# A transformer layer on one core: VectorE's batch work moved ahead of the low halves, seven batches of inverse roots moved to Pool, and ScalarE's copy of the value product moved behind the exponentials

## The chip, the cores and the metric

The kernel runs on one core of a Trainium2 chip. The metric is the device time of one execution in microseconds, a median over several executions. The engines are PE (matrix products), ACT (ScalarE), DVE (VectorE), POOL (GpSimd) and SP (SyncE, which here only issues transfers); each works through its own list in order, and semaphores tie the lists together.

## What is computed

A layer of attention and a mixture of experts over x of shape 8 x 512 x 128, 16 heads, a causal mask. Cut to what matters:

```
x = x + attention(layernorm(x))          # y = einsum(x, Wkqv) + bkqv; softmax(q k / sqrt(128), causal) v, then Wp, bp
x = x + experts(layernorm(x))            # a shared expert, and the top 2 of 8 by a sigmoid router
def layernorm(x, eps=1e-5): return (x - mean(x)) / sqrt(var(x) + eps)
```

## The kernel before, in words

`prepare` makes a folded 128 x 128 matrix per head and normalises the input. `body` runs one loop of slots t on every engine. A unit is one head of one batch: 8 batches x 16 heads are 128 units. Every engine's list is written slot by slot, and a table of numbers (`STEPS`, `PART_STEPS`) says in which slot each piece of rarer work stands.

In slot t of the attention part:

- PE projects unit t (`project`, L982 to L984, into bank 0), then does rare work (`after_attention`: the output product `proj` at L1074, the router's `logits` at L1096 and on, `count`, `rank`), then in every fourth slot the value product of four units (`weigh_values`, L1056), then scores of unit t - 10 (`score`, L1040 to L1042) in three pieces alternating with three pieces of the coarse scores of unit t - 1 (`score_for_max`, L1019). The coarse scores share two banks, so the third piece of a slot needs DVE to have finished with the first piece of the same slot.
- ACT copies the projection as `qh` (L1264), in slots of the value product copies that product out as `oT` (L1289), takes three exponentials of unit t - 10 (L1299), issues the store of `oT` (L1303), and has rare work: `rows<-hn` (L1252, the high half of the normalised rows), halves of expert weights (L1317), an exponential of the router's numbers.
- DVE makes the low half `ql` (L1399: the projection minus qh; it waits for qh, and PE's next projection waits for it), then `take_products` (which adds the output product to x, and makes the low half of hn at L1391), then three reductions of the coarse scores (L1427, `reduce_maxima`), then the rare work: `scale_weights` (L1476: low halves of expert weights), `after_attention` (statistics L1495, L1499, an inverse root by seed and Newton steps in 13 small instructions at L108 to L119 and L1506, the reciprocal `rinv` L1486) and `send_rows` (the router's sorting and ranking). In slots of the value product the rare work stands ahead of the reductions instead.
- POOL masks the exponentials of unit t - 10 (L914, L916), and then does rare work of the slot: `onT` (L937, the product of attention outputs and inverse sums, which `proj` needs) and `hn` (L944, four instructions, which ACT's `rows<-hn` needs), later indirect transfers.
- SP issues loads and stores in its own order. Every fourth slot it stores 16 rows `lowT` and loads them back into qh; once a batch it gathers attention outputs (L807, L808), stores and spreads the inverses (L812, L817), stores the rows (L821) and loads them transposed (L832), from which PE takes the logits.

I call a slot a value slot if t = 15 + 4g (`PV_AT`), a low slot if t = 6 + 4g (`LOW_AT`; PE turns the 16 rows there, L1215), and a plain slot otherwise. The numbers of `STEPS` count from slot 29 + 16 b of batch b, so steps 2, 6, 10 and 14 are value slots, 1, 5, 9 and 13 low slots, and the rest plain. The units end with slot 127, the scores with slot 137, and the experts' units start in slot 138.

Of the kernel before, what the change touches and what calls it, by code (L numbers as in the profile page):

```python
# [5 lines left out]
F32 = mybir.dt.float32  # L6
# [4 lines left out]
ALU = mybir.AluOpType  # L11
# [435 lines left out]
PV_AT = GROUP - 1 + LAG + 2  # L447
FFN_AT = UNITS + LAG
# [3 lines left out]
STEPS = {"rinv": 0, "mult": 2, "proj": 4, "stats": 6, "aggr": 6, "newton0": 6, "newton1": 7, "newton2": 7, "norm": 8, "split": 10, "logits": 14}  # L452
# [3 lines left out]
PART_STEPS = {"sort": 18, "weigh": 22, "count": 23, "rank": 26, "place": 26, "expert": 30, "send": 27}  # L456
LAST_PART_STEPS = {"sort": 9, "weigh": 10, "count": 11, "rank": 12, "place": 12, "expert": 13, "send": 13}
SORT_LATE = ((0, 0, 0, 1, 2, 3, 4), (0, 0, 0, 0, 1, 1, 1))


def step_at(name, b):

    if (name, b) == ("logits", B - 2):
        return step_at("rinv", b) - STEPS["rinv"] + LATE_LOGITS
    return PV_AT + H - GROUP + 2 + H * b + (STEPS if b < B - 1 else LAST_STEPS)[name]


def part_step_at(name, g):

    b = SPLITS[g][1] // TB - 1  # L470
    return step_at("rinv", b) - (STEPS if b < B - 1 else LAST_STEPS)["rinv"] + (PART_STEPS if b < B - 1 else LAST_PART_STEPS)[name]

# [31 lines left out]

W_MAX_AT, W_MAX_EVERY = 11, GROUP
# [3 lines left out]
W_SPLIT_AT, W_SPLITS = W_SHARED_AT + KINDS + 2, 2  # L509
# [7 lines left out]
def w_low_at(i):  # L517

    return W_SPLIT_AT + GROUP * (i // W_SPLITS) + W_SPLITS
# [167 lines left out]
def body(nc, m, ctx):  # L687
# [37 lines left out]
    var = sb("var2", [P, TB], F32)  # L725
    tmp = sb("tmp2", [P, TB], F32)
# [27 lines left out]
    def yg(t):  # L754
# [10 lines left out]
             "xn_ready", "xn_last_ready", "x_T", "ah_ready", "al_ready", "late_xh_ready", "late_sums_placed", "late_o_placed", "late_r_ready", "same_head_made", "v_done", "v_ready", "mh_ready", "ml_ready", "scale_chain")  # L765
# [7 lines left out]
     xn_ready, xn_last_ready, x_T, ah_ready, al_ready, late_xh_ready, late_sums_placed, late_o_placed, late_r_ready, same_head_made, v_done, v_ready, mh_ready, ml_ready, scale_chain) = (sem(n) for n in names)  # L773
# [15 lines left out]
    with nc.Block() as block:  # L789

        @block.sync
        def _(sp):
# [41 lines left out]
            for g in range(GROUPS):  # L834
# [841 lines left out]
```

## Time and profile before

| | us |
|---|---|
| median of 3 runs (731.1 to 735.19) | 731.4 |
| span of the profiled execution | 730.7 |
| attention, first unit to last (qh of slot 0 to qh of slot 127) | 29.2 to 502.3 |
| scores and value products left over | 502 to 540 |
| experts, last sums and stores | 532 to 730.7 |

The profile shows one execution. A row of the timeline gives the start, the duration, the engine, the source line, what is written and read, and in brackets how long the engine sat idle before and what ended it. PEclk is the clock that PE was granted as a share of 2.4 GHz, so 0.50 is 1.2 GHz.

### The profile page before, as it was taken

Reading aid. Unit: us, or ns where it says so; the run is one execution under the profiler, and the core shown is the slowest. Engines: PE = TensorE matmul, PEld = TensorE weight load, DVE = VectorE, ACT = ScalarE, POOL = GpSimd, SP = SyncE. Lnnn points to the kernel's source line nnn. Section 1 sums busy time; section 2 is a strip of 40 time slices with the busy share of each in tenths; the row PEclk is TensorE's granted clock in tenths of the full one; section 3 lists DMA queues with packets and bytes.
Section 4 is the critical chain, followed back from the end, with each engine's and each line's share of the span. In section 5 each row is a group of like instructions: output and inputs, shape, how many; then the busy total and the mean of one; then the engine's idle time right before and its main releaser. Section 6 shows DMA issues by size and latency. Waiting matters only on the chain.

```text
span 730.7 us, 16418 instructions
## 1 busy us (share of the span) xinstructions
PE 654.0 (90%) x5432; PEld 398.4 (55%) x5432; DVE 541.8 (74%) x1903; ACT 456.8 (63%) x816; POOL 310.2 (42%) x512
## 2 busy tenths in 40 slices
PE   7488999999999999998899999999986779899992
PEld 6264455545554554554445455455565568777652
DVE  6699877787788778788877877868546655567796
ACT  3376676767667776765676776666762545565651
POOL 4493531314123223221477522313465356565773
PEclk9699999999999999999999999999998889999997
DMA  9100443621122101221132111021444257695424
GB/s 255 53 2 20 133 128 105 175 77 45 49 74 44 32 32 42 77 70 37 49 93 85 45 51 42 17 44 64 102 107 107 73 117 145 126 164 120 110 60 126
DMA packets 102768, 60.24 MB, mean 82 GB/s; under 512 B 44568, under 2 KB 94640, under 8 KB 102688
## 3 DMA queue, kind: packets, MB, share of 16 engines
q1 hardware_dynamic: 66144, 28.22, 16.2%
q10 hardware_dynamic: 32336, 22.29, 10.4%
q0 software_dynamic: 4208, 8.69, 4.6%
q8 instruction: 47, 0.77, 0.4%
q14 instruction: 33, 0.27, 0.1%
HBM read 19.62 MB, written 30.77 MB: 69 GB/s over the span
## 4 chain that ended last, share of the span: by engine, by line
PE 63%; DVE 17%; ACT 6%; issue 6%; another core or an unknown queue 2%; POOL 1%; ACTq 0%; DVEq 0%; POOLq 0%
PE bank L1019 8%; PE bank L1040 7%; PE bank L1056 7%; PE bank L1042 6%; PE bank L1041 6%; DVE junk L1427 5%; PE bank L1136 4%; PE bank L1138 4%; PE bank L1137 4%; PE bank L982 3%; PE bank L984 3%; PE bank L983 3%; DVE ql L1399 3%; ACT p_sb L1299 2%
## 5 line engine op out<-in xcount | busy, mean ns | idle before, releaser
L1299 ACT ACTIVATE p_sb<-bank,inv_scale 128x512 f32<-128x512 f32 (+1 forms) x384 | 222.0, 614 | 40.6 <-PE bank L1042 33.3
L1427 DVE CUSTOM_DVE_ANT_0 junk<-bank,causal 128x512 bf16<-128x512 f32 (+3 forms) x512 | 221.8, 483 | 31.4 <-PE bank L1019 29.0
L914 POOL TENSOR_SCALAR_AFFINE_SELECT p_sb<-p_sb 128x384 f32<-128x384 f32 x128 | 67.0, 524 | 306.5 <-ACT p_sb L1299 305.9
L1041 PE MATMUL bank<-ql,ah 128*128 128x512 f16 (+3 forms) x512 | 153.4, 300 | 0.0
L1042 PE MATMUL bank<-qh,al 128*128 128x512 f16 (+3 forms) x512 | 153.0, 300 | 0.0
L1019 PE MATMUL bank<-ah,qh 128*128 128x512 f16 (+3 forms) x512 | 132.5, 303 | 21.8 <-DVE low L1427 20.3
L1040 PE MATMUL bank<-qh,ah 128*128 128x512 f16 (+3 forms) x512 | 147.2, 300 | 0.8 <-ACT p_sb L1299 0.8
L1399 DVE TENSOR_TENSOR ql<-bank,qh 128x512 f16<-128x512 f32 x128 | 88.5, 691 | 64.7 <-ACT qh L1264 61.3
L1264 ACT ACTIVATE qh<-bank 128x512 f16<-128x512 f32 x128 | 76.5, 597 | 62.4 <-PE bank L984 60.3
L1611 DVE SCALAR_TENSOR_TENSOR al<-bank,gu_scale,ah 128x512 f32<-128x512 f32 x69 | 51.6, 748 | 61.3 <-ACT ah L1330 41.9
L1019 PEld LDWEIGHTS bank<-ah,qh 128*128 128x128 f16 x512 | 50.1, 98 | 79.7 <-DVE low L1427 47.6
L1330 ACT ACTIVATE ah<-bank,inv_gate 128x512 f32<-128x512 f32 x69 | 47.4, 686 | 68.9 <-PE bank L1138 40.9
L962 POOL DMA_INDIRECT p_sb<-ys_dram,place x64 | 69.9, 1092 | 37.2 <-PE bank L1138 14.2
L953 POOL DMA_INDIRECT xs_dram<-rows,place x64 | 65.6, 1025 | 42.4 <-issue 14.4
L1056 PE MATMUL bank<-p_sb,v_sb 128*9 128x512 f32 (+3 forms) x1024 | 74.9, 433 | 0.3 <-POOL p_sb L916 0.3
L1040 PEld LDWEIGHTS bank<-qh,ah 128*128 128x128 f16 x512 | 50.2, 98 | 40.8 <-issue 8.3
L1042 PEld LDWEIGHTS bank<-qh,al 128*128 128x128 f16 x512 | 50.1, 98 | 25.0 <-issue 0.3
L1136 PE MATMUL bank<-mh,wh 128*128 128x256 f16 x212 | 60.3, 284 | 3.3 <-issue 1.6
L1138 PE MATMUL bank<-mh,wl 128*128 128x256 f16 x212 | 60.2, 284 | 2.1 <-issue 2.0
L1041 PEld LDWEIGHTS bank<-ql,ah 128*128 128x128 f16 x512 | 50.2, 98 | 21.7 <-issue 0.3
L1137 PE MATMUL bank<-ml,wh 128*128 128x256 f16 x212 | 60.0, 283 | 1.7 <-issue 1.7
L1174 PE MATMUL bank<-wh,qh 128*128 (+1 forms) x276 | 53.6, 227 | 6.3 <-ACT ql L1325 2.7
(247 smaller groups left out, 1130.2 us busy)
## 6 DMA issues: line engine op xcount, KB each, us to landing
o_dram<-oT ACTq DMA_DIRECT2D x32, 256.0 KB, 2.3
ys_dram<-ql ACTq DMA_DIRECT2D x25, 256.0 KB
xs_dram<-causal ACTq DMA_DIRECT2D x6, 832.0 KB, 4.8
wst<-in_Wkqv SPq DMA_DIRECT2D x8, 264.0 KB, 5.0
x_sb<-in_x SPq DMA_DIRECT2D x8, 256.0 KB, 5.8
out<-x_sb SPq DMA_DIRECT2D x8, 256.0 KB
o_all<-o_dram SPq DMA_DIRECT2D x7, 256.0 KB
r_all<-r_dram SPq DMA_DIRECT2D x7, 256.0 KB
```

The lines of the kernel that those rows point to most:

```text
L1019: last = nc.tensor.matmul(m.psum[M_BANK[n % 2]][:, at:at + w], qh[:, u % RING, i * P:(i + 1) * P], m.ah[:, seg(b, N, w)], start=True, stop ...
L1040: nc.tensor.matmul(bank, m.ah[:, keys], qh[:, s, c * P:N], start=True, stop=False)
L1041: nc.tensor.matmul(bank, m.ah[:, keys], ql[:, s, c * P:N], start=False, stop=False)
L1042: last = nc.tensor.matmul(bank, m.al[:, keys], qh[:, s, c * P:N], start=False, stop=True)
L1056: last = nc.tensor.matmul(m.psum[O_BANK][32 * j:32 * j + V1, c * P:N], m.v_sb[:, v // H * TB + c, v % H, :], p_sb[v % P_RING][:, P_AT[c]:P ...
L1136: nc.tensor.matmul(out, hi, x_h, start=True, stop=False)
L1137: nc.tensor.matmul(out, hi, x_l, start=False, stop=False)
L1138: return nc.tensor.matmul(out, lo, x_h, start=False, stop=True)
L1264: nc.scalar.activation(qh[:, t % RING, :], m.psum[Q_BANK][:, :], ACT.Copy).then_inc(qh_ready, 1)
L1299: nc.scalar.activation(p_sb[v % P_RING][:, S_AT[k]:S_AT[k] + S_WIDTH[k]], m.psum[S_BANK[k]][:, 0:S_WIDTH[k]], ACT.Exp, scale=m.inv_scale[: ...
L1399: nc.vector.tensor_tensor(ql[:, t % RING, :], m.psum[Q_BANK][:, :], qh[:, t % RING, :], ALU.subtract).then_inc(ql_ready, 1)
L1427: last = nc.vector.tensor_tensor_reduce(out=junk[:, (3 * u + k) % 2, at:at + w], in0=m.psum[M_BANK[(3 * u + k) % 2]][:, at:at + w], in1=m. ...
```

## The change

Six edits, all in the attention part:

1. DVE's rare work (`scale_weights`, `after_attention`, `send_rows`, the new `place_rows`) stands ahead of `ql` in every slot, where it stood behind the reductions (or, in value slots, between `ql` and the reductions).
2. The table puts a batch's pieces into other slots: rinv 0 to 3, mult (POOL's onT) 2 to 5, proj 4 to 6, stats 6 to 7, aggr 6 to 8, norm (POOL's hn) 8 to 9; split stays at 10, logits at 14. The router's pieces are dealt over more slots.
3. For batches 0 to 6 the 13 small DVE instructions of the inverse root give way to two on POOL, an addition and a power, ahead of hn.
4. ACT copies oT behind the three exponentials of a value slot, and issues its store right behind that.
5. ACT's halves of expert weights (24 in all, two to a group of four slots) move from a plain and a low slot to a low and a value slot; DVE's low halves of them move from a value slot (two at once) to the two plain slots behind it.
6. SP gathers the attention outputs behind the store of lowT instead of ahead of it, and spreads the inverses behind the load.

The value product is cut by a table of pieces that has one piece, so it stays whole and in its slot. The diff, cut:

```diff
+PV_PIECES = ((0, 1, 2, 3),)
+PV_LAST = len(PV_PIECES) - 1
...
 PLACE_LATE = -(-(PV_AT - LOW_AT) // GROUP)
-STEPS = {"rinv": 0, "mult": 2, "proj": 4, "stats": 6, "aggr": 6, "newton0": 6, "newton1": 7, "newton2": 7, "norm": 8, "split": 10, "logits": 14}
+STEPS = {"rinv": 3, "mult": 5, "proj": 6, "stats": 7, "aggr": 8, "newton0": 8, "newton1": 9, "newton2": 9, "norm": 9, "split": 10, "logits": 14}
...
-PART_STEPS = {"sort": 18, "weigh": 22, "count": 23, "rank": 26, "place": 26, "expert": 30, "send": 27}
-LAST_PART_STEPS = {"sort": 9, "weigh": 10, "count": 11, "rank": 12, "place": 12, "expert": 13, "send": 13}
-SORT_LATE = ((0, 0, 0, 1, 2, 3, 4), (0, 0, 0, 0, 1, 1, 1))
+PART_STEPS = {"sort": 15, "weigh": 24, "count": 23, "rank": 26, "slots": 27, "place": 28, "expert": 30, "send": 28}
+LAST_PART_STEPS = {"sort": 9, "weigh": 10, "count": 11, "rank": 12, "slots": 12, "place": 12, "expert": 13, "send": 13}
+SORT_LATE = ((0, 1, 3, 4, 5, 5, 7), (0, 0, 0, 0, 1, 1, 1))
...
-W_SPLIT_AT, W_SPLITS = W_SHARED_AT + KINDS + 2, 2
+W_SPLIT_AT, W_SPLITS = W_SHARED_AT + KINDS + 3, 2
...
-    return W_SPLIT_AT + GROUP * (i // W_SPLITS) + W_SPLITS
+    return W_SPLIT_AT + GROUP * (i // W_SPLITS) + W_SPLITS + i % W_SPLITS
...
-                if g >= PLACE_LATE and (g - PLACE_LATE) % PER_BATCH == PER_BATCH - 1:
-                    gather_products((g - PLACE_LATE) // PER_BATCH)
-                    spread_inverses((g - PLACE_LATE) // PER_BATCH)
                 sp.wait_ge(t_taken, T_TURN["low", g] + 1)
                 sp.dma_start(m.c_dram[g * GROUP * TB:(g + 1) * GROUP * TB, :], lowT[g % 2][:, :]).then_inc(low_stored, 16)
+                gathered = (g - PLACE_LATE) // PER_BATCH if g >= PLACE_LATE and (g - PLACE_LATE) % PER_BATCH == PER_BATCH - 1 else None
+                if gathered is not None:
+                    gather_products(gathered)
...
+                if gathered is not None:
+                    spread_inverses(gathered)
...
+                    pool.wait_ge(spread_known, b + 1)
+                    nc.gpsimd.tensor_scalar(pool_var[:, :], m.stats[:, seg(b, TB), 1], EPS, None, ALU.add).then_inc(var_raised, 1)
+                    pool.wait_ge(var_raised, b + 1)
+                    nc.gpsimd.tensor_tensor(m.rstd[:, seg(b, TB)], pool_var[:, :], minus_half[:, :], ALU.pow).then_inc(rstd_ready, 1)
...
-                if (g := group_at(t, PV_AT)) is not None:
-                    weigh_values(g)
+                if pieces_at(t):
+                    weigh_values(*pieces_at(t))
...
-                if (g := group_at(t, PV_AT)) is not None:
-                    act.wait_ge(pv_done, g + 1)
-
-                    if g >= 2:
-                        act.wait_ge(o_stored[g % 2], 16 * (g // 2))
-                    nc.scalar.activation(oT[g % 2][:, :], m.psum[O_BANK][:, :], ACT.Copy).then_inc(oT_ready, 1)
...
-                if (g := group_at(t, PV_AT)) is not None:
+                if (g := weighed_at(t)) is not None:
+                    act.wait_ge(pv_done, g + 1)
+                    if g >= 2:
+                        act.wait_ge(o_stored[g % 2], 16 * (g // 2))
+                    nc.scalar.activation(oT[g % 2][:, :], m.psum[O_BANK][:, :], ACT.Copy).then_inc(oT_ready, 1)
                     act.wait_ge(oT_ready, g + 1)
                     act.dma_start(m.o_dram[g * P:(g + 1) * P, :], oT[g % 2][:, :]).then_inc(o_stored[g % 2], 16)
...
+                    if b < B - 1:
+                        last.then_inc(spread_known, 1)
+                    else:
+                        post.link(last)
+                        rsqrt_seed(nc, post.link, m.stats[:, seg(b, TB), 1], var[:, :], m.rstd[:, seg(b, TB)], tmp[:, :])
...
-                    if (b := batch_at(f"newton{step}", t)) is not None:
+                    if (b := batch_at(f"newton{step}", t)) == B - 1:
...
-                if (g := part_at("rank", t)) is not None:
+                if (g := part_at("slots", t)) is not None:
...
+
+            def place_rows(t):
+                c = sort
                 if (g := part_at("place", t)) is not None:
...
-                attend(t)
-                if group_at(t, PV_AT) is None:
+                if t < FFN_AT:
+                    scale_weights(t)
+                    after_attention(t)
+                    send_rows(t)
+                    place_rows(t)
+                    attend(t)
                     reduce_maxima(t)
-                scale_weights(t)
-                feed_forward(t - FFN_AT)
-                if t >= FFN_AT:
+                else:
+                    feed_forward(t - FFN_AT)
                     take_products(t)
-                after_attention(t)
-                send_rows(t)
-                if group_at(t, PV_AT) is not None:
-                    reduce_maxima(t)
+                    after_attention(t)
+                    send_rows(t)
+                    place_rows(t)
```

Three places of the order. First ACT at the value slot 35 (batch 0, step 6), from the copy qh of that slot to the copy qh of the next; before:

```order
L1264 ACTIVATE qh<-bank 128x512
L1289 ACTIVATE oT<-bank 128x512
L1299 ACTIVATE p_sb<-bank,inv_scale 128x512 x2
L1299 ACTIVATE p_sb<-bank,inv_scale 128x256
L1303 DMA o_dram<-oT 128x512
L1264 ACTIVATE qh<-bank 128x512
```

and now:

```order
L1295 ACTIVATE qh<-bank 128x512
L1324 ACTIVATE p_sb<-bank,inv_scale 128x512 x2
L1324 ACTIVATE p_sb<-bank,inv_scale 128x256
L1330 ACTIVATE oT<-bank 128x512
L1332 DMA o_dram<-oT 128x512
L1295 ACTIVATE qh<-bank 128x512
```

The copy oT stood ahead of the exponentials; now it and its store stand between the last exponential and the next qh.

Second POOL in batch 0, where p_sb0 to p_sb7 are the exponentials of units by their number modulo 8 (each slot masks one unit, so here p_sb0 is slot 34, p_sb1 slot 35, p_sb3 slot 37, p_sb4 slot 38 and p_sb5 slot 39). Before, from slot 37 on:

```order
L914 AFFINE_SELECT p_sb3<-p_sb3 128x3x128
L916 AFFINE_SELECT p_sb3<-p_sb3 128x128
L944 TENSOR_SCALAR hn<-x_sb,stats,rstd 128x128 x4
L914 AFFINE_SELECT p_sb4<-p_sb4 128x3x128
L916 AFFINE_SELECT p_sb4<-p_sb4 128x128
L914 AFFINE_SELECT p_sb5<-p_sb5 128x3x128
```

and now, from slot 34 on (p_sb0):

```order
L942 AFFINE_SELECT p_sb0<-p_sb0 128x128
L963 TENSOR_TENSOR onT<-o_all,r_all 128x512
L940 AFFINE_SELECT p_sb1<-p_sb1 128x3x128
...
L942 AFFINE_SELECT p_sb4<-p_sb4 128x128
L966 TENSOR_SCALAR pool_var<-stats 128x4
L968 TENSOR_TENSOR rstd<-pool_var,minus_half 128x4
L974 TENSOR_SCALAR hn<-x_sb,stats,rstd 128x128 x4
L940 AFFINE_SELECT p_sb5<-p_sb5 128x3x128
```

hn stood behind the masks of slot 37, two slots ahead of its reader; it stands behind those of slot 38, one slot ahead. onT, which stood in slot 31, stands behind the masks of slot 34, one slot ahead of PE's output product.

Third PE in the value slot 35 now, from the scores of slot 34 to the value product (before, the output product stood two slots earlier, in the plain slot 33):

```order
L1049 MATMUL bank2<-ah,qh 128x256
L1012 MATMUL bank0<-ah,mh 128x512
L1013 MATMUL bank0<-al,mh 128x512
L1014 MATMUL bank0<-ah,ml 128x512
L1105 MATMUL bank7<-wp,onT 128x128 x4
L1086 MATMUL bank6<-p_sb4,v_sb 9x512
```

The output product, which waits for onT, stands ahead of the value product and of the scores of its slot.

## Rows read from the trace of the kernel before

**Rows 1.** The page, first part: busy time of each engine, its share of the span, instructions.

```profile
PE 654.0 (90%) x5432; PEld 398.4 (55%) x5432; DVE 541.8 (74%) x1903; ACT 456.8 (63%) x816; POOL 310.2 (42%) x512
```

**Rows 2.** Windows, the fourth of six batches (slots 77 to 92) and the sum of six.

```profile
310.99:377.26 66.27, 60.24 (x461) 31.47 (x460) 54.74 (x219) 43.00 (x78) 24.26 (x45) 0.97 0.20 59
sum 364.84, PE 351.14 PEld 185.77 DVE 287.95 ACT 251.89 POOL 124.00; mean PE 58.52 PEld 30.96 DVE 47.99 ACT 41.98 POOL 20.67
```

**Rows 3.** Waits: total us, times, longest.

```profile
DVE ql L1399 <- ACT qh L1264: 61.3, 106, 1.5
```

**Rows 4.** Timeline of ACT, value slot 63 and plain slot 64.

```profile
257.61 0.60 ACT L1264 ACTIVATE qh<-bank 128x512 f16<-128x512 f32 x1
...
262.10 0.47 ACT L1299 ACTIVATE p_sb<-bank,inv_scale 128x256 f32<-128x256 f32 x1
262.81 0.60 ACT L1264 ACTIVATE qh<-bank 128x512 f16<-128x512 f32 x1 [0.25 <-PE bank L984]
...
265.76 0.60 ACT L1264 ACTIVATE qh<-bank 128x512 f16<-128x512 f32 x1 [0.38 <-PE bank L984]
```

**Rows 5.** Timeline of DVE and PE, slot 64: first reduction's end, third coarse score.

```profile
264.66 0.08 DVE L1427 DVE_READ_ACCUMULATOR2_ANT low<- 128x1 f32 x1
...
264.80 0.28 PE L1019 MATMUL bank<-ah,qh 128*128 128x256 f16 x1
```

**Rows 6.** Timeline of DVE and ACT, plain slot 69, rare work ahead of ql.

```profile
281.74 0.30 DVE L116 SCALAR_TENSOR_TENSOR tmp<-rstd,var 128x4 f32<-128x4 f32 x1
...
281.81 0.60 ACT L1264 ACTIVATE qh<-bank 128x512 f16<-128x512 f32 x1 [0.38 <-PE bank L984]
...
282.86 0.69 DVE L1399 TENSOR_TENSOR ql<-bank,qh 128x512 f16<-128x512 f32 x1
...
285.18 0.60 ACT L1264 ACTIVATE qh<-bank 128x512 f16<-128x512 f32 x1 [0.40 <-PE bank L984]
```

**Rows 7.** Timeline of POOL (slots 62, 63, 69) and PE's output product of slot 65.

```profile
257.70 0.29 POOL L916 TENSOR_SCALAR_AFFINE_SELECT p_sb<-p_sb 128x128 f32<-128x128 f32 x1
...
263.37 1.27 POOL L937 TENSOR_TENSOR onT<-o_all,r_all 128x512 f32<-128x512 f32 x1
...
265.56 0.83 PE L1074 MATMUL bank<-wp,onT 128*128 128x128 f32 x6
...
285.21 3.13 POOL L944 TENSOR_SCALAR hn<-x_sb,stats,rstd 128x128 f32<-128x128 f32 x4
```

**Rows 8.** Timeline of ACT, slots 135 and 139.

```profile
526.05 0.63 ACT L1252 ACTIVATE rows<-hn 128x512 f16<-128x512 f32 x1 [2.31 <-POOL hn L944]
...
539.46 0.36 ACTq L1303 DMA_DIRECT2D o_dram<-oT  x1
539.86 0.69 ACT L1330 ACTIVATE ah<-bank,inv_gate 128x512 f32<-128x512 f32 x1 [0.43 <-issue]
```

**Rows 9.** Timeline of SP and PE, slots 71 to 75: weight load, transposed load, logits.

```profile
291.05 0.36 SPq L794 DMA_DIRECT2D xl<-in_gate_w  x1
...
296.70 1.26 SPq L832 DMA_TRANSPOSE xl<-x_dram  x1
...
302.36 0.17 PE L1096 MATMUL bank<-rwh,xh 128*128 128x8 f16 x1
```

**Rows 10.** Groups of DVE by line and shape: count, busy, mean ns.

```profile
L1476 DVE SCALAR_TENSOR_TENSOR wl<-xh,w_scale,wh 128x256 f16<-128x256 f32 x12 | 5.7, 506 | 0.0
...
L1525 DVE RECIPROCAL pr<-ex 128x96 f32<-128x96 f32 x2 | 1.5, 754 | 0.1
```

**Rows 11.** Timeline and windows of PE (us, busy, clock) at two waits.

```profile
62.27 0.28 PE L1019 MATMUL bank<-ah,qh 128*128 128x256 f16 x1 [1.49 <-DVE low L1427]
...
62.27:63.27 1.00, 1.00 (x6) 1.00 0.00 0
...
339.82 0.39 PE L1019 MATMUL bank<-ah,qh 128*128 128x256 f16 x1 [2.51 <-DVE low L1427]
...
340.00:343.00 3.00, 3.00 (x9) 0.50 0.00 0
```

More of the change, by code:

```diff
@@ L502, in group_at, with pieces_at, weighed_at @@
     return g if r == 0 and 0 <= g < GROUPS else None
+def pieces_at(t):
+    if t == PV_AT + GROUP * (GROUPS - 1):
+        return GROUPS - 1, tuple(range(TB))
+    g, r = divmod(t - PV_AT, GROUP)
+    return (g, PV_PIECES[r]) if 0 <= g < GROUPS - 1 and r < len(PV_PIECES) else None
+def weighed_at(t):
+    return GROUPS - 1 if t == PV_AT + GROUP * (GROUPS - 1) else next((g for g in range(GROUPS - 1) if t == PV_AT + GROUP * g + PV_LAST), None)
 W_MAX_AT, W_MAX_EVERY = 11, GROUP
@@ L725, in body @@
     var = sb("var2", [P, TB], F32)
+    pool_var = sb("pool_var", [P, TB], F32)
+    minus_half = sb("minus_half", [P, TB], F32)
     tmp = sb("tmp2", [P, TB], F32)
@@ L764, in body @@
              "half_added", "out_ready", "out_stored",
[L765 removed]
+             "xn_ready", "xn_last_ready", "x_T", "ah_ready", "al_ready", "late_xh_ready", "late_sums_placed", "late_o_placed", "late_r_ready", "same_head_made", "spread_known", "var_raised", "v_done", "v_ready", "mh_ready", "ml_ready", "scale_chain")
     (q_done, qh_ready, ql_ready, max_scored, max_ready, low_stored, low_placed,
@@ L772, in body @@
      half_added, out_ready, out_stored,
-     xn_ready, xn_last_ready, x_T, ah_ready, al_ready, late_xh_ready, late_sums_placed, late_o_placed, late_r_ready, same_head_made, v_done, v_ready, mh_ready, ml_ready, scale_chain) = (sem(n) for n in names)
+     xn_ready, xn_last_ready, x_T, ah_ready, al_ready, late_xh_ready, late_sums_placed, late_o_placed, late_r_ready, same_head_made, spread_known, var_raised, v_done, v_ready, mh_ready, ml_ready, scale_chain) = (sem(n) for n in names)
     o_stored = [sem(f"o_stored{k}") for k in range(2)]
@@ L885, in _ @@
             nc.gpsimd.memset(low[1][:, :], 0.0).then_inc(low_clear, 1)
+            nc.gpsimd.memset(minus_half[:, :], -0.5).then_inc(low_clear, 1)
+            pool.wait_ge(low_clear, 3)
             def spread_x(b):
@@ L1043, in score, with weigh_values @@
                 last.then_inc(s_done, 1)
-            def weigh_values(g):
-                pe.wait_ge(p_masked, 2 * GROUP * (g + 1))
-                if g >= 1:
-                    pe.wait_ge(oT_ready, g)
-                else:
-                    pe.wait_ge(o_clear, 1)
-                for c in range(TB):
+            def weigh_values(g, pieces):
+                if pieces[0] == 0:
+                    pe.wait_ge(p_masked, 2 * GROUP * (g + 1))
+                    if g >= 1:
+                        pe.wait_ge(oT_ready, g)
+                    else:
+                        pe.wait_ge(o_clear, 1)
+                for c in pieces:
                     w = N - c * P
@@ L1057, in weigh_values @@
                                                 start=(c == 0), stop=(c == TB - 1), skip_group_check=True)
-                last.then_inc(pv_done, 1)
+                if pieces[-1] == TB - 1:
+                    last.then_inc(pv_done, 1)
             def turn(name, n):
```

11 lines of the change are left out of this document (6 added, 5 removed).

## The prediction

> **What bounds the kernel now.** I began with the busy shares: PE is busy 90% of the span, DVE 74% [rows 1], so PE sets the pace unless another engine hands it something late. How late that is I read from windows over the six full batches, slots 29 to 124, a window a batch: 364.84 us, in which PE was busy 351.14, so it stood still for 13.7 us, and 6.0 of these fall into one batch, slots 77 to 92 [rows 2]. That 13.7 us, plus what a low clock cost once (below), is all that a better placed DVE can give back here. Then I read single slots in the timeline. A value slot lasts 262.81 - 257.61 = 5.20 us and a plain one 265.76 - 262.81 = 2.95 [rows 4]. Three slacks in them carry the argument.
> DVE waits for qh 61.3 us in 106 slots, 0.58 us each [rows 3]: that is the room for work ahead of ql. An overrun isn't caught up: in slot 69 DVE worked from 281.74 to 282.86 (1.12 us) ahead of ql, ql began 1.05 behind qh, and the slot took 3.37 us, 0.42 more than 2.95 [rows 6]. Up to about 0.7 us is free, the rest is paid in full.
> PE wants the third coarse score of a plain slot at 264.80, and DVE releases its bank at 264.74 [rows 5]: 0.06 us. So a qh that is late by x makes ql, the reduction and then PE late by x - 0.06.
> ACT waits 0.25 us for PE before the qh behind a value slot [rows 4]. It has no more than that there.
>
> **The change, part by part** (offsets are from the start of the named slot's qh).
> *oT behind the exponentials.* Ahead of them the copy cost nothing, since the scores weren't there yet. Behind them, ACT ends the last exponential at about 262.48 (262.10 + 0.47, less the overlap of copies in a row) [rows 4], copies for 0.60, and must then see the copy done before it issues the store. What that takes is in the trace once: ACT idle for 0.43 us behind such a store, laid to issue [rows 8]. So the next qh starts at 262.48 + 0.60 + 0.43 = 263.5 in place of 262.81, 0.67 late, 0.6 for PE. There are 28 value slots from 15 to 123; 6 are priced apart below. 22 x 0.6 = 13.2 us. Bounds: 0 if the slot behind absorbs it, 0.7 each if nothing does.
> *Halves of expert weights on ACT.* 12 of the 24 now stand in value slots, behind the store; the like instruction on DVE takes 0.51 us [rows 10] and ACT's is of that size. ACT has no room left there: 12 x 0.5 = 6.0 us. In the slots where they stood they fitted.
> *onT one slot ahead of the output product.* In a low slot POOL ends its masks at 257.70 + 0.29 = 257.99, 0.38 behind the next qh (257.61) [rows 4, 7]. onT takes 1.27 [rows 7], so it is there at +1.67. PE wants it 0.20 ahead of that qh: 265.56 against 265.76 [rows 4, 7]. PE stands 1.67 + 0.20 = 1.87 us, with value product and scores behind it, so nothing hides it. 6 batches: 11.1 us.
> *hn one slot ahead of ACT's rows.* The masks end at +0.38. Then come the addition and the power, which the trace doesn't show. Below, each takes no less than the shortest instruction of the rows, 0.08 us [rows 5]; above, no more than POOL's product of 128x512, 1.27 us [rows 7]. I take 0.3 each, since they have four elements a partition, much nearer the low end. hn takes 3.13 [rows 7]: ready at +4.1. ACT makes rows to +4.75 (0.63 [rows 8]), and only then its three exponentials (about 1.75 us, a short one being 0.47 [rows 4]), oT (0.6) and the store (0.4): +7.5 in place of +5.20. DVE goes the same way, waiting for the rows in front of its reductions, and would end them at about +7.15. 2.3 us per batch, with oT's delay in it, 13.8 us. That such waits happen the trace shows where hn was late once: ACT idle 2.31 us [rows 8]. In the other batches hn came in time.
> The Trainium skill ("GPSIMD Engine Reference", Engine selection) speaks against this move: elementwise work belongs on VectorE, GpSimd being about twice as slow. DVE's small instructions here take 0.15 to 0.30 us [rows 6]; twice that gives 0.3 to 0.6 us each for POOL's two, as an estimate by that page, and up to 4 us more over seven batches than I sum.
> *A later weight load.* SP issues expert 3's load when the low half before it is done, which was in slot 71 and is now in slot 73, and the transposed load of batch 2 stands behind it. From the load (291.05) to the second transpose's end of issue (297.96) is 6.9 us [rows 9], from slot 73's qh + 0.5 now; PE wants the result 5.9 us behind that qh (a plain and a low slot, less 0.2). With about 2 us to land that is some 3 us of stall, once; bounds 1.5 and 5.
> *DVE.* Off it come 13 small instructions for each of seven batches, at 0.15 to 0.30 us each [rows 6] some 3 us a batch, half of which already ran behind a value product. The 0.42 us of slot 69 [rows 6] and its likes in the other batches, part of the 13.7 us, go to nothing. What stays: slots 77 to 92 now put routing pieces of 0.5 to 1.5 us (the reciprocal alone is 0.75 [rows 10]) with a low half of 0.5 in front of ql in plain slots that have 0.7. I add up 4.5 us there, 2.7 in the others. Of 13.7 + 1.6 us, 7.2 stay: -8.1 us. Bounds: 0 and -15.
> *Hidden.* The gather and the spread on SP come later, but from rinv to onT there are now two plain slots and a low one, 9 us, where the value slot and a plain one were enough. The same count in the tail, slots 128 to 137: the seventh onT and the seventh hn, about 3.5 us together.
> **Sum:** 13.2 + 6.0 + 11.1 + 13.8 + 3.0 - 8.1 + 3.5 = 42.5 us. The profiled execution's span was 730.7 us, the median 731.4; on the median that is **774 us**.
>
> **Rivals.**
> *The clock falls as well.* A wait of PE of 2.51 us was followed by three microseconds at 0.50, the level of 1.2 GHz, and one of 1.49 us was not: clock 1.00 behind it [rows 11]. At half clock 3.2 us of PE's work take 3.2 us more, of which half is lost against full speed: 1.6 us. My new waits, 1.9 us at the output product and about 1.8 in the slot of the rows, lie between the two. The skill's page "TensorE: Matmul & The Clock Gate" (HAM oscillation) has it that waits in a matmul stream, if long enough, put the clock down each time. If it falls at all 14, that is 22 us: 796 us. A dear power on POOL leads here too. In its favour: the waits are alike, so they fall together or not. Against: 1.49 is nearer. Chance 0.21, and 0.05 for still more.
> *The lateness overlaps.* POOL's, ACT's and DVE's delays each fall into slots with a value product; if onT and hn come earlier than I read (for instance since ACT's exponentials of low slots run ahead once PE waits), only the first two terms and the load stay: 731.4 + 13.2 + 6.0 + 3.0 - 8.1 = 745 us. Against it: POOL's masks wait for the exponentials in every slot. Chance 0.13.
> *DVE's gain decides, faster.* If PE stands in for ACT, that is, if a qh 0.67 us late cost nothing, because DVE's room ahead of ql moves with it, and onT and hn came in time, the DVE term alone would be left: 731.4 - 8 = 723 us, at best 716. The point from which it decides: the six other terms must be under 8 us, a fifth of what I read. Chance 0.06.
> *It does nothing,* gain and loss equal, within 1%: 0.04.
>
> **Chances and range.** 0.51 for the forecast (its own range 758 to 786), 0.26 above, 0.13 at about 745, 0.10 at or below 739. The range that leaves out no more than 2 in 10 takes in the lower rival and the clock's case: 743 to 797. A measurement of this kernel tells some 1% from no change. Faster by over 1%: 0.06; within 1%: 0.04; slower by over 1%: 0.90.
>
> **What would show each step.** ACT's oT without idle in front of it and the next qh 0.6 to 0.7 us later, and the plain slot behind a value slot at 3.5 us: first step. A wait of PE's output product for POOL's onT of about 1.9 us, seven times: third. ACT's rows waiting for hn about 3.5 us, and value slots of step 10 at 7.5: fourth, and the power's duration with it. PE waiting for the logits' input once in batch 2: fifth. DVE's ql waiting less than 61 us in total, and slots 77 to 92 still the longest batch: sixth. PEclk at 0.5 in short pieces in every batch would show the clock rival. I'm wrong if the value slots keep 5.20 us, or if POOL's masks run early.

## The result and the profile after

The changed kernel takes 795.4 us, median of 4 runs (789.0 to 801.2), the kernel before beside it 732.6 (731.1 to 735.2). The ratio is 1.0824, 95% interval 1.077 to 1.0878. The profiled execution has a span of 791.6 us against 730.7: 60.9 us more. Of runs over 1.5% above their kernel's fastest, none is in a ratio here or below: 801.2 us here, one of 839 and one of 3681 us on the second chip. The forecast was 774 (743 to 797), 42.5 us more. The measured time is inside the range but above the forecast's own 758 to 786; it lies at the upper end, where I had put the rival in which the clock falls at every new wait.

The page of the kernel after, engines' busy time; of before it is [rows 1].

```profile
PE 669.2 (85%) x5432; PEld 401.4 (51%) x5432; DVE 525.9 (66%) x1812; ACT 448.3 (57%) x816; POOL 320.4 (40%) x527
```

DVE lost 15.9 us of work and is idle more, as all engines are. PE has 15 us more busy time with the same matmuls, most of it the lower clock (below).

Windows of the kernel after: the same six batches as in [rows 2], each from the qh of its step 0 to the next. Columns: the stretch, its length, busy time and instructions of PE, PEld, DVE, ACT, POOL, then PEclk, DMA share, GB/s.

```profile
133.70:200.26 66.56, 59.92 (x457) 31.22 (x456) 45.20 (x168) 39.18 (x70) 17.91 (x39) 0.97 0.25 73
...
267.58:343.44 75.86, 64.62 (x457) 32.12 (x456) 46.32 (x171) 42.46 (x78) 18.60 (x39) 0.91 0.13 40
343.44:413.62 70.18, 58.91 (x461) 31.09 (x460) 51.86 (x205) 42.13 (x78) 24.56 (x45) 1.00 0.19 55
...
sum 414.36, PE 362.82 PEld 188.01 DVE 277.89 ACT 245.24 POOL 133.46; mean PE 60.47 PEld 31.34 DVE 46.31 ACT 40.87 POOL 22.24
```

The six batches take 414.36 us in place of 364.84. PE stands still for 51.5 of them (414.36 - 362.82) where it was 13.7 [rows 2], and is busy 11.7 longer. So 49.5 of the 60.9 us are in these slots, 2.2 in the slots ahead of them, and 9.0 behind slot 127 (from its qh to the end 237.4 us, before 228.4).

Now the places. First ACT's timeline in value slot 63 and behind it, the kernel after:

```profile
278.51 0.60 ACT L1330 ACTIVATE oT<-bank 128x512 f32<-128x512 f32 x1
279.13 0.33 ACTq L1332 DMA_DIRECT2D o_dram<-oT  x1
279.51 0.51 ACT L1346 ACTIVATE wh<-xh,w_scale 128x256 f16<-128x256 f32 x1 [0.40 <-ACT oT L1330]
279.92 0.58 ACT L1295 ACTIVATE qh<-bank 128x512 f16<-128x512 f32 x1
```

These are the copy, 0.40 us in which the store is issued, a half of weights, and only then the qh that PE has long made possible (there is no idle time of its own in front of it). Before, a wait of 0.25 us for PE stood there [rows 4].

Then the output product of value slot 35, on PE and on POOL:

```profile
155.09 1.26 POOL L963 TENSOR_TENSOR onT<-o_all,r_all 128x512 f32<-128x512 f32 x1
...
156.50 1.13 PE L1105 MATMUL bank<-wp,onT 128*128 128x128 f32 x8 [1.79 <-POOL onT L963]
```

and the rows of slot 39, on POOL and ACT (its qh starts at 172.62):

```profile
172.98 0.24 POOL L966 TENSOR_SCALAR pool_var<-stats 128x4 f32<-128x4 f32 x1
173.30 1.05 POOL L968 TENSOR_TENSOR rstd<-pool_var,minus_half 128x4 f32<-128x4 f32 x1
174.46 3.15 POOL L974 TENSOR_SCALAR hn<-x_sb,stats,rstd 128x128 f32<-128x128 f32 x4
...
177.65 0.63 ACT L1283 ACTIVATE rows<-hn 128x512 f16<-128x512 f32 x1 [4.43 <-POOL hn L974]
```

The waits of the whole program for these two, and DVE's for qh (before: [rows 3]); total, times, longest:

```profile
DVE ql L1428 <- ACT qh L1295: 59.5, 95, 1.8
...
ACT rows L1283 <- POOL hn L974: 31.8, 7, 5.4
...
PE bank L1105 <- POOL onT L963: 13.8, 7, 3.0
```

Batch 2's logits, PE:

```profile
330.43 0.17 PE L1127 MATMUL bank<-rwh,xh 128*128 128x8 f16 x1 [3.06 <-DMA xl<-x_dram]
```

And the clock, PE's windows behind four of these waits:

```profile
156.00:157.00 1.00, 0.50 (x4) 1.00 0.01 4
157.00:158.00 1.00, 1.00 (x12) 1.00 0.08 16
...
180.00:183.00 3.00, 3.00 (x12) 0.54 0.62 191
...
249.00:252.00 3.00, 2.94 (x20) 1.00 0.76 183
...
330.00:336.00 6.00, 5.57 (x46) 0.50 0.01 1
```

Behind the 1.79 us of slot 35 (ended at 156.50) the clock stays at 1.00. Around the end of a wait of 2.64 us, at 179.66, it goes to the lower level, 1.2 GHz, for about 3.4 us; behind one of 2.61 ended at 248.28 it doesn't; at the 3.06 us of the logits it does, for 6.8. In the attention of all profiles here such a fall lasts 3.4 or 6.8 us, and I count 6.8 as two pieces. There are seven pieces in the attention now, in four of the six batches, and there was one before. If PE would have been busy in all of them, (7 - 1) x 3.4 / 2 = 10.2 us are lost, at most. Behind slot 127 it is 32.0 us at the lower level where it was 25.9, at most 3.1 us lost.

### The profile page after: what moved, and what is told of

Read it like the earlier page. It is cut to its first block, busy times and chain, and to the rows that moved or that the text cites. A ratio compares the mean times of both kernels' runs of the same rounds, so it can differ in the third digit from the quotient of the medians.

```text
span 791.6 us, 16335 instructions
## 1 busy us (share of the span) xinstructions
PE 669.2 (85%) x5432; PEld 401.4 (51%) x5432; DVE 525.9 (66%) x1812; ACT 448.3 (57%) x816; POOL 320.4 (40%) x527
## 4 chain that ended last, share of the span: by engine, by line
PE 53%; DVE 14%; ACT 11%; POOL 8%; issue 7%; another core or an unknown queue 1%; ACTq 1%; DMA 1%; SPq 0%; DVEq 0%; POOLq 0%
PE bank L1086 8%; PE bank L1049 6%; ACT p_sb L1324 5%; PE bank L1070 5%; PE bank L1072 5%; PE bank L1071 5%; DVE junk L1456 5%; PE bank L1169 3%; PE bank L1167 3%; PE bank L1168 3%; DVE ql L1428 3%; POOL hn L974 3%; PE bank L1012 2%; PE bank L1014 2%; PE bank L1013 2%
## 5 line engine op out<-in xcount | busy, mean ns | idle before, releaser
L1324 ACT ACTIVATE p_sb<-bank,inv_scale 128x512 f32<-128x512 f32 (+1 forms) x384 | 218.1, 613 | 120.9 <-PE bank L1072 118.6
L1086 PE MATMUL bank<-p_sb,v_sb 128*9 128x512 f32 (+3 forms) x1024 | 82.1, 464 | 0.3 <-POOL p_sb L942 0.3
```

The source lines that it names most:

```text
L1086: last = nc.tensor.matmul(m.psum[O_BANK][32 * j:32 * j + V1, c * P:N], m.v_sb[:, v // H * TB + c, v % H, :], p_sb[v % P_RING][:, P_AT[c]:P ...
L1324: nc.scalar.activation(p_sb[v % P_RING][:, S_AT[k]:S_AT[k] + S_WIDTH[k]], m.psum[S_BANK[k]][:, 0:S_WIDTH[k]], ACT.Exp, scale=m.inv_scale[: ...
```

## The experiments

A part was undone in the changed kernel, or done alone in the kernel before. The runs came on two chips. The first, that of the result, has the kernel before at 732 to 735 us, the second at 702; each ratio is to the kernel before on its own chip. I give microseconds of difference in the text, and the length of batches from the profiles, which is the same on both chips but for falls of the clock (below).

**Undoing one part.** *oT ahead of the exponentials again*, the store left behind them:

```diff
+                if (g := weighed_at(t)) is not None:
+                    act.wait_ge(pv_done, g + 1)
...
+                    nc.scalar.activation(oT[g % 2][:, :], m.psum[O_BANK][:, :], ACT.Copy).then_inc(oT_ready, 1)
                 v = t - LAG
...
                 if (g := weighed_at(t)) is not None:
-                    act.wait_ge(pv_done, g + 1)
...
-                    nc.scalar.activation(oT[g % 2][:, :], m.psum[O_BANK][:, :], ACT.Copy).then_inc(oT_ready, 1)
                     act.wait_ge(oT_ready, g + 1)
```

> The changed kernel (795 us) with one edit undone: ACT copies oT ahead of the three exponentials of a value slot again, the store stays behind them. Theory: the copy and its store delay the next qh by 0.70 us in every value slot, in 22 of the 28 without cover (in the six slots of the output product PE stands for onT anyway, and the trace shows 1.80 us there in all). Expected: value slots at 5.20 us, 15 us less, about 780. Rival (PE's waits put the clock down and cost most of it; the copy is covered by them): 0 to 3 us less, about 793.

Measured: 786.0 us, ratio 1.0682 (1.0647 to 1.0716): about 10 us less than the changed kernel. Value slots at steps 2 and 14, which were 0.69 to 0.80 us too long, are back to their old length in the batches without other work. In the profile the six batches and the slots ahead of them are 11.7 us shorter although one more piece of low clock fell into them (1.7 us), so 13.4 without it. The size of the term holds; the rival (0 to 3 us) is out. The value slots alone gained more than that, but the plain slots behind them are longer than in the changed kernel, by up to 1.0 us each without any fall of the clock (the run of the four together shows why).

*onT a slot earlier:*

```diff
-STEPS = {"rinv": 3, "mult": 5, ...
+STEPS = {"rinv": 3, "mult": 4, ...
```

> The changed kernel with POOL's onT at step 4 in place of 5, two slots ahead of the output product. PE waits 1.8 us for it in each of six batches now. If the waits stand beside the delay of oT: 6 x 1.8 = 11 us less, 784. If the wait covers the 0.7 us of oT in the same slot, as the steps of the trace say (1.80 in all), that comes out again: 6 x 1.1 = 7 us less, 789. Clock theory: two of the seven waits at this place were followed by 3.4 us at half clock, so another 3 us less.

Measured: 783.3 us, ratio 1.064 (1.0585 to 1.0695): 12 us less, or 13 to 14 by the ratios. PE's waits for onT are gone in the six batches (the seventh, behind the last unit, is still there). Step 6 of batch 0 went from 2.87 us over its length with an output product in it (5.97 us) to 0.83, so the wait cost its full 2.0 us and oT's 0.8 stood beside it. I had read "1.80 in all" as an overlap and forgot that DVE's old overrun of 1.07 us in that slot, part of the 13.7 of [rows 2], had gone at the same time. The first of the two sums, 11 us, was right; the batches fell by 11.1 us with one piece of low clock more. The further 3 us from the clock did not come: the falls came at other waits.

*hn a slot earlier:*

```diff
-STEPS = {..., "norm": 9, "split": 10, ...
+STEPS = {..., "norm": 8, "split": 10, ...
```

> The changed kernel with POOL's addition, power and hn at step 8 in place of 9, two slots ahead of ACT's rows. The slot of the rows is 2.9 to 3.3 us longer than before, of which 0.7 is oT's. Expected: that slot back to 5.9 us, ACT's wait of 4.4 us for hn gone or under 2.5 (no scores are there before that), 6 x 2.3 = 14 us less and up to 3 us more by two clock falls: about 780. Rival: the power, which took 1.04 us where I had 0.3, still makes hn late two slots ahead: then 6 x 0.5 to 1 us stay.

Measured: 776.1 us, ratio 1.0556 (1.0529 to 1.0584): 19 to 20 us less. ACT's wait for hn in the six batches is 0.4 to 1.4 us now, in a time in which no scores are there, and step 10 is 0.7 over its old length, which is oT's. In the profile 2.2 us less at this place in each batch, and three pieces of low clock in the attention instead of seven. This was the dearest of the three parts undone one by one on this chip, with four pieces of low clock less in its profile.

*The four together,* with ACT's halves of weights a slot earlier:

```diff
-W_SPLIT_AT, W_SPLITS = W_SHARED_AT + KINDS + 3, 2
+W_SPLIT_AT, W_SPLITS = W_SHARED_AT + KINDS + 2, 2
```

> The changed kernel with the four suspected parts undone together: oT ahead of the exponentials, onT at step 4, POOL's addition, power and hn at step 8, ACT's weight halves one slot earlier (and with them expert 3's load). What stays of the change: DVE's work ahead of ql, the power on POOL, the router's table, the order on SP. Theory: the terms are complete, so it is the kernel before less DVE's gain: 731.4 - 8 = 723 us, and one fall of the clock in the attention at most. Rival: something else of the change costs (the move ahead of ql, the order on SP): 731 to 745 us.

Measured: 736.7 us (10 runs), before 734.9, ratio 1.0024 (1.0001 to 1.0047). So the four parts are about 59 us of the change, and what is left of it gives no gain: the rival holds, something else costs. Measured against its own kernel before, that is 10 us beside my expectation, and the profile says where. Windows of this kernel, its six batches, sum:

```profile
sum 360.57, PE 349.49 PEld 185.86 DVE 278.14 ACT 252.24 POOL 135.92; mean PE 58.25 PEld 30.98 DVE 46.36 ACT 42.04 POOL 22.65
```

That is only 4.3 us less than before, and 1.1 less than the profile of the kernel before that has no fall of the clock (361.68 us, second chip). DVE's timeline at plain slot 85 (batch 3, step 8) of this kernel, the end of the rare work ahead of ql:

```profile
343.24 0.23 DVE L1579 TENSOR_SCALAR top<-top,inv_down 128x12 f32<-128x12 f32 x1
343.50 0.25 DVE L1581 TENSOR_TENSOR weight<-top 128x12 f32<-128x12 f32 x2
343.79 0.69 DVE L1429 TENSOR_TENSOR ql<-bank,qh 128x512 f16<-128x512 f32 x1
```

The slot's qh started at 342.58 and ql could have started at 343.21, but comes at 343.79. In single plain slots DVE's pieces now cost 0.3 to 1.3 us each. Most of this wasn't in the changed kernel. The slots right behind a value slot (steps 3, 7, 11 and 15) are 7.4 us too long in all in these six batches; in the changed kernel they are 2.9, half of it by falls of the clock. Slot 52 (batch 1, step 7), ACT's qh and DVE's ql, the changed kernel and then this one:

```profile
231.82 0.60 ACT L1295 ACTIVATE qh<-bank 128x512 f16<-128x512 f32 x1 [0.46 <-PE bank L1072]
...
232.55 0.67 DVE L1428 TENSOR_TENSOR ql<-bank,qh 128x512 f16<-128x512 f32 x1
```

```profile
218.00 0.60 ACT L1295 ACTIVATE qh<-bank 128x512 f16<-128x512 f32 x1 [0.25 <-PE bank L1014]
...
219.43 0.67 DVE L1429 TENSOR_TENSOR ql<-bank,qh 128x512 f16<-128x512 f32 x1
```

In both, DVE has the same 1.5 us of rare work ahead of ql. In the changed kernel the qh behind a value slot is late, so half of that work is done when it starts; ql begins 0.73 us behind qh and the slot is hardly longer (0.08 us). Here qh isn't late, ql begins 1.43 behind it, and the slot is 0.78 us too long. So the parts don't add up one by one: the late qh hid DVE's overruns, and undoing it brought them out.

Behind slot 127 this kernel is 7.1 us longer than before: ACT's first expert activation comes 35.6 us behind the last qh in place of 31.2 (the seventh hn is 2.8 us later), and PE is at the lower clock for 35 us there in place of 26. This is one profile of each kernel, and runs of the kernel before on this chip differ by up to 6 us among themselves.

*ACT's halves alone* (that last edit alone, on the changed kernel):

> The changed kernel with ACT's halves of expert weights one slot earlier (a plain and a low slot again); DVE's low halves of them then stand in the value slot and the plain slot behind. Expert 3's load stands ahead of batch 2's transposed load two slots earlier. Theory: the stall of 3.1 us at batch 2's logits goes, with the fall of the clock behind it (7.6 us in all in that batch), and the halves' 0.3 us in 12 value slots: 10 to 11 us less, about 784. Rival: the load isn't what delays the transposed load: only 3 to 4 us less.

Measured on the second chip: 757.9 us, ratio 1.0785 (1.0757 to 1.0812), 55.6 us over the kernel before, where the changed kernel was 62.8 over it on the first. Batch 2 took 67.72 us in place of 75.86, 8.1 less: PE's wait of 3.06 us at the logits is gone, and so are three of the four pieces of low clock in that batch (at most 5.1 us). With the edit SP issues expert 3's load in slot 72 in place of 73, and the transposed load behind it in slot 73 in place of 75: the load's place was the cause. Three pieces of low clock more fell elsewhere. Across two chips and with random falls I call the 10 us neither confirmed nor refuted; the stall itself is shown.

**Doing one part alone, in the kernel before.** *oT behind the exponentials:*

> The kernel before with one part of the change alone: ACT copies oT behind the three exponentials of a value slot and issues its store right behind. Here no wait of PE covers it in the six slots of the output product. Theory: 0.70 us in each of 28 value slots, 20 us more than before, about 752, with DVE's overruns of up to 1 us in some value slots covering a part: not under 745. Rival (overlap): under 10 us.

Measured: 719.4 us, ratio 1.0236 (1.0211 to 1.0261): 17 us more. ACT in value slot 47, this kernel:

```profile
206.79 0.60 ACT L1300 ACTIVATE oT<-bank 128x512 f32<-128x512 f32 x1
207.42 0.33 ACTq L1302 DMA_DIRECT2D o_dram<-oT  x1
...
207.85 0.60 ACT L1264 ACTIVATE qh<-bank 128x512 f16<-128x512 f32 x1 [0.46 <-ACT oT L1300]
```

Without any wait for POOL the next qh comes 5.89 us behind the last, not 5.20. Three of a batch's four value slots pay 0.69 to 0.80 us in most batches; the fourth, at step 6, mostly pays nothing, since DVE is up to 1.07 us over there and covers it. That is why it is 17 and not 20.

*The power on POOL,* hn kept at step 8:

> The kernel before with one part of the change alone: for batches 0 to 6 POOL's addition and power (0.24 and 1.04 us in the changed kernel) in place of DVE's 13 instructions; POOL's hn keeps step 8, everything else is as it was. Theory: DVE's rare work in a value slot is free up to some 2.4 us between ql and the reductions; at step 6 it was 3.3 (1.07 us over), of which the seed was 1.15, and the rest of the inverse root cost 0.43 in step 8. Expected: steps 6 and 8 without loss, 1.3 us a batch and 2 to 3 in batch 3, together 9 to 10 us less than before, about 725. Rival: hn ready 1.4 us later on POOL makes rows late, 0 or slower.

Measured: 700.5 us, before 702.3, ratio 0.9979 (0.9962 to 0.9995). Of the 9 to 10 us that I expected 2 came. Steps 6 and 8 lost next to nothing any more, as expected, but for 1.1 us at step 6 of batch 3. But POOL's hn is 1.9 us or more later in the six batches (1.5 in batch 6), ACT waits for it in every batch, and step 10 becomes 0.5 to 0.6 us too long in three batches, and 3.8 in batch 3 (1.6 before), where PE waited 2.8 us and the clock fell. In batch 6 it is worse. ACT's rows there, of this kernel and of the kernel before on the same chip:

```profile
520.41 0.63 ACT L1260 ACTIVATE rows<-hn 128x512 f16<-128x512 f32 x1 [3.77 <-POOL hn L952]
```

```profile
523.81 0.63 ACT L1252 ACTIVATE rows<-hn 128x512 f16<-128x512 f32 x1 [2.30 <-POOL hn L944]
```

A wait of 3.77 us in place of 2.30; the first expert activation comes 34.2 us behind the last qh, not 31.1.

*The power on POOL and the router's table* (the last run's edits, with the sorts spread, the weights' low halves one by one in a value slot and a plain slot):

```diff
-PART_STEPS = {"sort": 18, "weigh": 22, "count": 23, "rank": 26, "place": 26, "expert": 30, "send": 27}
+PART_STEPS = {"sort": 18, "weigh": 24, "count": 23, "rank": 26, "place": 28, "expert": 30, "send": 29}
-SORT_LATE = ((0, 0, 0, 1, 2, 3, 4), ...
+SORT_LATE = ((0, 0, 0, 2, 3, 4, 4), ...
-    return W_SPLIT_AT + GROUP * (i // W_SPLITS) + W_SPLITS
+    return W_SPLIT_AT + GROUP * (i // W_SPLITS) + W_SPLITS + i % W_SPLITS
```

> power_alone with the router's pieces and the weights' low halves laid so that a value slot has at most 2.7 us of DVE's rare work (between ql and the reductions) and a plain slot about 0.6: sorts 0, 0, 0, 2, 3, 4, 4 behind step 18, weigh 24, place 28, send 29, one low half of weights in the value slot and one in the plain slot behind it. Theory: batch 3 loses some 5 us in power_alone and under 2 here, so 3 to 4 us less than power_alone, about 721. Rival: single plain slots over 0.6 us give it all back: same as power_alone.

Measured: 701.7 us, ratio 0.9986 (0.9971 to 1.0001). Batch 3 went from 64.50 to 60.88 us as expected, but batch 2 from 58.53 to 64.37: a low half one slot later puts expert 3's load into slot 73, where it was in 71, and PE waits 3.4 us at the logits. It is the changed kernel's stall, made again by another edit, and gone again when the low halves stay in place (below). The rival, single plain slots, shows only in two low slots, 0.5 us each.

**The second chip.**

> The kernel before, unchanged, for its trace on the same chip as the next three. The runs of power_alone and its neighbours had the kernel before at 702.3 us where the others had 732 to 735. Theory: the slots of the attention have the lengths known (5.20, 2.95, 3.13 us, batches 59.5, 60.7, 59.5, 66, 60, 58.6) on either chip, and all of the difference lies behind slot 127. Rival: a clock that is higher all through, with shorter slots.

The kernel before took 702.7 us. The six batches are 59.48, 60.69, 59.45, 63.96, 59.48 and 58.62 us, on the first chip 59.49, 60.71, 59.46, 66.27, 60.27 and 58.64 (one fall of the clock in the fourth). From slot 127 on it is another matter. Windows of the kernel before, 580 to 620 us, on the first chip and then on the second:

```profile
580.00:620.00 40.00, 33.67 (x345) 28.56 (x346) 24.11 (x57) 18.66 (x33) 19.56 (x19) 0.91 0.61 125
```

```profile
580.00:620.00 40.00, 39.82 (x483) 36.91 (x481) 28.65 (x54) 28.77 (x50) 29.01 (x29) 1.00 0.95 177
```

On the second chip more is moved in these 40 us, 177 GB/s against 125, and PE stands still for 0.2 us in place of 6.3. Of the 29.8 us between the two spans (730.7 and 700.9) 27.6 lie behind slot 127. The theory holds in the main: the slots of the attention have the same length. Why the later stage is faster on one chip stays open; there is one profile of each.

**Mended.** *The power and hn at step 7, and batch 6 as it was, in the kernel before* (shown against the kernel with the power alone):

```diff
+    if name == "norm" and b < B - 2:
+        return PV_AT + H - GROUP + 2 + H * b + POWER_STEP
...
+                    if b < B - 2:
+                        pool.wait_ge(spread_known, b + 1)
...
-                    if (b := batch_at(f"newton{step}", t)) == B - 1:
+                    if (b := batch_at(f"newton{step}", t)) is not None and b >= B - 2:
```

> power_alone with two things mended that its trace showed: POOL's addition, power and hn at step 7 (in power_alone, at step 8, the slot of the rows was 0.5 to 0.6 us long in three batches and 3.8 in batch 3), and batch 6 keeps its inverse root on DVE (there the experts began 1.8 us later behind the last unit). Theory: the attention is 11 us shorter than before and nothing is lost behind it: ratio 0.985. Rival: the gain is given back behind slot 127, whatever is done in the attention (the experts wait for transfers): ratio 0.995 or above.

Measured: 693.1 us, before 702.2, ratio 0.989 (0.985 to 0.993). The six batches are 353.35 us, 8.3 less, where I expected 11 in the attention, and behind slot 127 nothing is given back (198.7 us, before 200.9): the rival is out.

*And the router's table, low halves as before:*

> power_step7 with the router's pieces spread (sorts 0, 0, 0, 2, 3, 4, 4 behind step 18, weigh 24, place 28, send 29), the weights' low halves left as they were before, so that no load is late. Theory: batch 3 loses 3 to 4 us in power_step7 and 2 to 3 here: 1 us less, ratio 0.983. Rival: the later sends of rows delay the experts: slower than power_step7.

Measured: 692.8 us, ratio 0.9871 (0.9833 to 0.9909). Windows of this kernel, six batches, sum:

```profile
sum 352.85, PE 348.29 PEld 185.81 DVE 276.46 ACT 252.72 POOL 131.85; mean PE 58.05 PEld 30.97 DVE 46.08 ACT 42.12 POOL 21.97
```

The batches take 352.85 us, against 361.68 of the kernel before on this chip, with 4.6 us of idle PE left; four of the six are at 58.0 to 58.3. The gain of 8.8 us arrives in the time (9.3). Both kernels give it; between them (0.989 and 0.9871) nothing can be told, and of the 1 us that I expected from the table 0.5 shows in batch 3. This kernel is faster than the kernel before by 1.3% (0.9 to 1.7), and than the changed kernel by about 9% (0.9871 against 1.0824). DVE at step 6 of batch 0, this kernel:

```profile
155.01 0.94 DVE L1454 TENSOR_REDUCE w_max<-xh 128x3 f32<-128x768 f32 x1
155.87 0.86 DVE L1507 BATCH_NORM_STATS2 bn<-x_sb 128x6 f32<-128x128 f32 x4
156.65 0.36 DVE L1511 BATCH_NORM_AGGREGATE stats<-bn 128x2 f32<-128x6 f32 x4
```

2.0 us of rare work, between ql and the reductions, cost nothing: in a value slot PE is in the value product then. In the kernel before 1.3 us of the inverse root followed here, and the slot was 1.07 too long. The changed kernel gave this pocket up and put all of it ahead of ql, where 0.6 us are free.

*The inverse root back on DVE, in the changed kernel:*

> The changed kernel with the inverse root back on DVE for all batches (seed at step 8, the steps at 9, ahead of ql), POOL has only hn at step 9. Theory: hn starts right behind POOL's masks and is there 1.45 us earlier, 6 x 1.4 = 9 us less, but DVE has 1.5 us of work ahead of ql in slot 8 and 0.9 in slot 9 where 0.6 to 0.7 are free, which costs 6 x 1.2 = 7 us: within 3 us of the changed kernel, the ratio to the kernel before at 1.075 to 1.085. Rival: the power is the dear part: 9 us less in full, ratio 1.07.

Measured: 760.9 us, ratio 1.0839 (1.0772 to 1.0905). The same as the changed kernel within its interval; the six batches are 3.5 us shorter, with two pieces of low clock less. hn starts right behind the masks, and step 10 of batch 0 is 1.22 us over instead of 3.56, but step 8 is 0.98 over and step 9 0.24. That is 2.4 us in all, against 2.88 at the changed kernel's step 10 in a batch without a fall of the clock: the power saves DVE about what it costs POOL. Where it stands is what matters.

## Why the prediction was right, point by point, and what it missed

1. **oT and store, 13.2 us.** Right: 0.70 us a slot where I had 0.6, in 22 slots 15 to 16 us; undoing it gave 13.4 us in the profile with the clock evened out. One sign that I had named for it was wrong: the plain slot behind a value slot stays at 2.95 us and isn't 3.5, the value slot itself is longer.
2. **Halves of weights, 6.0.** Somewhat high: value slots with a half are 1.05 us over, those without 0.70, so 0.35 each in place of 0.5, 4 us in all. The half runs 0.51 us, but the next qh starts 0.10 before its end, and the gap ahead of it is 0.40 where without a half it is 0.46.
3. **onT, 11.1.** Right: waits of 1.74 to 1.91 us in six batches where I had worked out 1.87, and 11 to 13 us by the run.
4. **hn, 13.8.** Right in kind, with a term too small: addition and power took 0.24 and 1.04 us, not 0.3 each, and hn was ready 5.0 us behind the qh, not 4.1. ACT waited 4.4 us for it, not 3.5, and the slots were 2.9 us over in the batches without a half there and without a fall of the clock (1 and 5), where I had 2.3: 17 us in all. The Trainium skill ("GPSIMD Engine Reference", Engine selection) gives the factor of two for operations with two inputs, and about line rate for those with one, which the prediction left out. The addition has one input and took 0.24 us where the like one on DVE took 0.17 before, in between; the power has two and took more than the 0.3 to 0.6 us of that estimate.
5. **The load ahead of batch 2's logits, 3.0.** Right: 3.06 us, and two pieces of low clock with it (3.4 us), which I had not priced.
6. **DVE, -8.1.** Right for the changed kernel. Against the kernel before without a fall of the clock (361.68 us) the six batches are 52.7 us longer. Of these oT is 13.3 (18 value slots), the halves 4.2, onT 12.2, hn 17.3 with oT's delay in it, the load 3.1 and the seven pieces of low clock 10 to 12 us; that leaves -7 to -9 for DVE. But the reason wasn't in my sum: a good part of it is owed to the late qh, which hides DVE's work in the slot behind; my third rival had that as a condition (DVE's room ahead of ql moves with a late qh), the forecast had not. With the other parts undone 1.1 of it is left. The pocket of some 2.2 us between ql and the reductions of a value slot (3.31 us of rare work at step 6 of batch 0 made it 1.07 too long) wasn't in my sum either: the change gives it up, and with qh in time the pieces overrun in plain slots instead.
7. **Behind slot 127, 3.5.** Too small: 9.0 us, at most 3.1 of them the clock. The seventh onT costs PE 2.98 us, and ACT waits 5.44 for the seventh hn, in place of 2.31 [rows 8].
8. **The clock.** The rival's mechanism came to about half its size: falls at 5 of the 12 new waits of the batches, 3.4 us each, and two pieces at the logits; batches 3 and 4 have none. A piece costs at most 1.7 us, where I had 1.6 (from a sentence that says 3.2 us more and means half of it). At most 10 us were lost in the attention, up to 3 behind it. It is the largest part of what the 42.5 us lacked; the others are terms 4, 7 and 1. I had set the forecast at none and the rival at all, with nothing between. That the time came within a microsecond of the rival's 796 is chance: half of its clock, and the rest from terms that were too small.

Sum of what was found: oT 16, halves 4, onT 12, hn 17, load 3, DVE -8, behind slot 127 without the clock 6, clock 12 to 13, about 62 against 60.9 us.

Over all profiles of this case I counted the waits of PE in the attention, at full clock ahead of them, by length, and after how many the clock fell (the lower level began during the wait or within 1.5 us of its end):

| wait of PE | fell | did not |
|---|---|---|
| 1.2 to 1.6 us | 0 | 29 |
| 1.6 to 2.2 us | 12 | 21 |
| 2.2 to 2.8 us | 18 | 11 |
| over 2.8 us | 8 | 0 |

The longest wait without a fall is 2.79 us, and the next longer one, 2.81, has a fall, so the last bound runs close between the two; most of these waits stand at a few places of like kernels. So my rival's question, whether 1.9 us would behave like 1.49 or like 2.51 [rows 11], was put wrongly: in between it falls sometimes. The 2.51 us itself is a case of it: the kernel before waits 2.50 us at the same place on the second chip, and the clock doesn't fall. Undoing oT's place left most waits at the output product and the rows as they were, and the falls came at others of them. What decides it at one of these places stays open. The changed kernel's runs spread over 12 us and those before over 4, but the kernel with hn at step 8, which has three pieces, spreads over 0.9: the spread shows nothing of the clock. The Trainium skill ("TensorE: Matmul & The Clock Gate", HAM oscillation) tells of a kernel in which every wait for a transfer, of some 3 to 5 us, put the clock down again; the eight waits over 2.8 us here agree with it, and for the shorter ones the counts stand by themselves.

## What to carry to other kernels

Where engines go in lock-step, price a moved instruction by what is free at the new place and by what was free at the old one: here the pocket behind ql in a value slot was nearly four times the room ahead of ql (2.2 and 0.6 us). The kernel that gave it up gained 1.1 us in six batches, the one that kept it 8.8; they differ in the router's slots too, so the pocket's share isn't measured alone. Costs of moved work needn't add up: one engine's lateness hid another's overrun, which came out when the lateness was taken away. A producer put one slot ahead of its reader must be checked with all that stands in front of it in its own engine's list; for onT two slots were enough and one was not, and for hn with the power ahead of it only three slots left no wait. A cheaper instruction on another engine pays only if its result is needed later than it gets there: the same power with its hn gave 0.2% at one step and 1.1% at the step before, there without batch 6.

## What the runs showed of the hardware

- The power on POOL takes 1.04 to 1.05 us for 4 elements a partition, in all seven places, near the 1.26 us of a product of 128x512; an addition of the same size 0.24.
- Between ACT's copy and ACT's next instruction 0.40 to 0.46 us pass when the store of the copy is issued there.
- The table above: of 62 waits of PE of 1.6 to 2.8 us, 30 came with a fall of the clock and 32 without, the same wait at the same place (2.5 us) once each way. A fall in the attention lasted 3.4 or 6.8 us.
- Two chips of this case differ by 4% on the same kernel, nearly all of it behind slot 127, where the experts' transfers are (125 and 177 GB/s from 580 to 620 us).
